# Bias rows copied into PSUM by ScalarE, the gain tables read as 32-row slices, and the order of VectorE and ScalarE changed in and ahead of the loop

## The reference

```
# layer 0
kx   = modulated_linear(x, s, k_aff_w, k_aff_b, k_w, k_b)     # per token 16 heads of 32
A    = softmax(kx kx^T / sqrt(32))                            # 16 x 16 heads, within a token
x    = x + modulated_linear(A kx, s, o_aff_w, o_aff_b, o_w, o_b)
# modulated_linear: w_mod = w * style, each row scaled to length 1; x w_mod^T + b
# layer 1, ln(x, g, b) is a layer norm with the gain and bias rows that the token's ids pick
h    = ln(ln(x, pw_g[pid], pw_b[pid]), cp_g[cid], cp_b[cid])
t, s = ln(x, tm_g[cid], tm_b[cid]), ln(x, ms_g[sid], ms_b[sid])
m, n, r = x + mlp_ln(memory), x + mlp_ln(noise), x + mlp_ln(resource)   # one row per batch
cat  = [w0*h, w1*t, w2*m, w3*n, w4*r, w5*s],  w = softmax(aw)
x    = x + ln(silu(cat @ int_W1 + int_b1) @ int_W2 + int_b2, int_g, int_be)
```

## Time and profile before

| | us |
|---|---|
| median of 3 runs | 938.13 |
| lowest, highest | 935.24, 938.22 |
| the profiled execution, its own time | 936.79 |
| its span, first to last instruction | 935.0 |
| TensorE busy | 876.8 (94%) |
| VectorE busy | 698.0 (75%) |
| GpSimd busy | 592.5 (63%) |
| ScalarE busy | 450.6 (48%) |

### The profile page before, as it was taken

The page is one execution under the profiler, slowest core; times in us unless marked ns, Lnnn a source line. Parts: engine busy times, 40 slices in busy tenths (PEclk is TensorE's granted clock), DMA queues, the critical chain, the costliest instruction groups (busy, mean ns, idle before and its releaser), DMA issues.

```text
span 935.0 us, 19902 instructions
## 1 busy us (share of the span) xinstructions
PE 876.8 (94%) x7518; PEld 789.8 (84%) x7566; DVE 698.0 (75%) x1129; ACT 450.6 (48%) x790; POOL 592.5 (63%) x742
## 2 busy tenths in 40 slices
PE   5876798999999999999999999999999999999987
PEld 5744697988989898998989898998979898999886
DVE  3679867778697777778787777778787777768642
ACT  3565336454544546454544645454544645453421
POOL 2267797766566675756576675856676675857551
PEclk9987799999999999999999999999999999999999
DMA  8951232422333232323334242323334242222110
GB/s 291 414 203 33 70 97 69 119 56 93 97 110 111 81 108 68 108 54 104 99 91 130 69 119 69 90 50 116 102 84 122 68 117 64 93 53 85 35 46 23
DMA packets 101871, 93.78 MB, mean 100 GB/s; under 512 B 72720, under 2 KB 75024, under 8 KB 100112
## 3 DMA queue, kind: packets, MB, share of 16 engines
q1 hardware_dynamic: 91984, 67.93, 24.0%
q0 software_dynamic: 4608, 16.78, 6.5%
q10 hardware_dynamic: 5184, 7.79, 2.7%
HBM read 67.83 MB, written 8.39 MB: 82 GB/s over the span
## 4 chain that ended last, share of the span: by engine, by line
PE 50%; DVE 26%; issue 9%; ACT 7%; another core or an unknown queue 4%; POOL 2%; DMA 2%; ACTq 1%; DVEq 0%; SPq 0%; POOLq 0%
PE acc L368 30%; PE tok L368 12%; PE att L368 3%; PE xp L511 3%; PE xp L368 2%; DVE norm L1280 2%; DVE ytmp L1266 2%; DVE SE L1195 2%; DVE small L1199 1%; DVE SE L1222 1%; DVE SE L1210 1%; DMA p_kb<-in_kb 1%; ACT pgb L795 1%; DVE alo L1228 1%
## 5 line engine op out<-in xcount | busy, mean ns | idle before, releaser
L1476 POOL TENSOR_TENSOR xlo<-xraw,xhi 128x512 fp32r<-128x512 f32 x32 | 46.8, 1464 | 104.8 <-ACT xhi L736 104.8
L1530 POOL TENSOR_TENSOR op1l<-ytmp,op1h 128x512 fp32r<-128x512 f32 x64 | 84.2, 1316 | 31.1 <-ACT op1h L824 30.7
L368 PE MATMUL acc<-op1h,W1th 128*128 128x256 f32 x256 | 80.2, 313 | 10.9 <-POOL op1l L1530 10.9
L368 PE MATMUL acc<-op0h,W1xh 128*128 128x256 f32 x256 | 77.2, 301 | 1.5 <-DVE op0l L1252 1.5
L824 ACT CAST op1h<-ytmp 128x512 fp32r<-128x512 f32 x64 | 39.7, 621 | 78.6 <-DVE ytmp L1266 78.6
L368 PE MATMUL acc<-op1h,W1hh 128*128 128x256 f32 x256 | 77.5, 303 | 0.0
L368 PE MATMUL acc<-op1l,W1th 128*128 128x256 f32 x256 | 77.4, 302 | 0.0
L368 PE MATMUL acc<-op1h,W1tl 128*128 128x256 f32 x256 | 77.3, 302 | 0.0
L368 PE MATMUL acc<-op0h,W1sh 128*128 128x256 f32 x256 | 73.7, 288 | 0.0
L368 PE MATMUL acc<-op0h,W1xl 128*128 128x256 f32 x256 | 73.0, 285 | 0.0
L368 PE MATMUL acc<-op0l,W1xh 128*128 128x256 f32 x256 | 73.0, 285 | 0.0
(11 more groups left out here) (248 smaller groups left out, 3201.2 us busy)
## 6 DMA issues: line engine op xcount, KB each, us to landing
xsq<-in_x SPq DMA_DIRECT2D x32, 256.0 KB, 4.3
xb<-in_x SPq DMA_DIRECT2D x32, 256.0 KB, 2.9
out<-xb SPq DMA_DIRECT2D x32, 256.0 KB, 2.0
xraw<-in_xT SPq DMA_DIRECT2D x31, 256.0 KB, 4.3
BD<-q SPq DMA_DIRECT2D x124, 64.0 KB, 2.1
BD<-v SPq DMA_DIRECT2D x124, 64.0 KB
ring<-in_k_wT ACTq DMA_DIRECT2D x12, 256.0 KB
ring<-in_o_wT ACTq DMA_DIRECT2D x12, 256.0 KB
```

The lines of the kernel that those rows point to most:

```text
L368: return e.matmul(o, a, b, start=start, stop=True, skip_group_check=True)
L1476: e.tensor_tensor(xlo[:, :, :], xraw[:, :, :], xhi[:, :, :].bitcast(F32), ALU.subtract).then_inc(s["xlo"], 1)
L1530: e.tensor_tensor(op[slot]["l"][:, :, half(g)], four(ytmp[YT[n, g][0]]), op[slot]["h"][:, :, half(g)].bitcast(F32), ALU.subtract).then_inc ...
```

## The change

1. **Bias rows.** In the 32 `W2_part`s and in `proj(g)` of the 14 even groups from 4 on, the bias matmul with `selT` is gone. ScalarE copies the row, held in SBUF for all partitions (`kb`, `b2`), into the PSUM bank ahead of the matmuls (`bias_q`, `bias_2`), which then all accumulate. The other 18 `proj`s keep theirs.
2. **Gain tables.** `gain_tables` and `GT` are gone. `gains` takes the 32 partitions of `tab` and of `OH` that hold its table: matmuls over 32 rows of the array.
3. **Steps with weights.** ScalarE's `z_copy(pb)` stands ahead of `mod_hi`, VectorE's `product(pb, "t")` ahead of `mod_lo`.
4. **Ahead of the loop.** VectorE's `vectors_end` is cut in two and moved behind `e_second(1)`; the three batch-row tables L are made by ScalarE straight from PSUM; `split3` for `PT` moves into step 1, between `q_T(b)` and `a_lo(a)`; its inputs `rp` and `t1` lie in other buffers, so groups 2 and 3 are loaded earlier and `gint` later. On TensorE `values(1)` comes ahead of `vec_T`, `a_T(1)` ahead of `tables_mnr`. GpSimd makes the later batches' row scales (`demod(., 1)`) ahead of the loop.

```diff
             def proj(g, kts=range(4)):
+
                 o = tok[1 if g else 0]
...
+                    elif on_bias:
+                        e.wait_ge(s["sd"], g // 2 - 1)
...
-                    three(o[:, :], xhi[:, kt, :], xlo[:, kt, :], WL["k", "h"][:, kt, :], WL["k", "l"][:, kt, :], kt == 0)
+                    i = three(o[:, :], xhi[:, kt, :], xlo[:, kt, :], WL["k", "h"][:, kt, :], WL["k", "l"][:, kt, :], kt == 0 and not on_bias)
                 if kts[-1] == 3:
-                    mm(o[:, :], selT[:, 0, :], tab[:, :]).then_inc(s["A"], 1)
+                    if not on_bias:
+                        i = mm(o[:, :], selT[:, :], tab[:, :])
+                    i.then_inc(s["A"], 1)
...
                 for c in range(4):
-                    i = mm(o[:, c * 128:c * 128 + 128], GT[n][:, c * 128:c * 128 + 128], OH[(g // 2) % 2][:, half(g)], start=(c == 0))
+                    i = mm(o[:, c * 128:c * 128 + 128], tab[q, c * 128:c * 128 + 128], OH[(g // 2) % 2][q, half(g)], start=(c == 0))
...
-            def W2_last(g):
-                W2_part(g, (2, 3))
-                mm(tok[g % 2][:, :], selT[:, 1, :], tab[:, :]).then_inc(s["W2"], 1)
...
+            def bias_q(g):
+
+                e.wait_ge(s["ql"], g)
+                e.copy(tok[1][:, :], kb[:, :]).then_inc(s["sd"], 1)
+
+            def bias_2(g):
+
+                if g % 2 == 0:
+                    e.wait_ge(s["x1"], min(g + 3, NG))
+                elif g < NG - 1:
+                    e.wait_ge(s["ql"], min(g + 4, NG))
...
+                e.copy(tok[g % 2][:, :], b2[:, :]).then_inc(s["sw"], 1)
...
+                if k > 1:
+                    z_copy(pb)
                 if mod:
                     mod_hi(*mod, (0, 1))
-                if k > 1:
-                    z_copy(pb)
                 prod_hi(pb, "t")
...
                     prod_hi(pb, "s")
+                    if more:
+                        bias_q(a + 2)
...
                     z_make(a)
+                    bias_2(pa)
                     sum_part(b, "S", "Sc")
                     if more:
                         q_hi(a + 2)
                     exponential(b)
+                    bias_2(pb)
...
+            vectors_norm()
+            e_T(1)
+            x_one(0)
+            e_second(1)
             vectors_end()
-            x_one(0)
-            e_T(1)
             q_lo(2)
-            e_second(1)
-            for n in "mnr":
-                table_rows(n)
...
-            split3(1, rp[:, :], PT[:, :])
...
+                product(pb, "t")
                 if mod:
                     mod_lo(*mod, (0, 1))
-                product(pb, "t")
...
                     q_T(b)
+                    if k == 1:
+                        split3(1, rp[:, :], PT[:, :])
                     a_lo(a)
```

More of the change, by code:

```diff
@@ L622, in _ @@
             proj(2)
+            values(1)
             vec_T()
-            values(1)
             z_T(0)
+            a_T(1)
             tables_mnr()
-            a_T(1)
             scores(2)
@@ L679, in _ @@
                     u_T(a)
-                W2_first(pa)
-                W2_first(pb)
-                W2_last(pa)
+                W2_part(pa, (0, 1))
+                W2_part(pb, (0, 1))
+                W2_part(pa, (2, 3))
                 if front:
@@ L686, in _ @@
                     scores(a + 2)
-                W2_last(pb)
+                W2_part(pb, (2, 3))
                 if front:
@@ L911, in _ @@
             q_hi(2)
+            e_first(1)
             z_make(0)
-            e_first(1)
             split_x(3)
             squares(3)
+            sum_part(1, "AV", "AVc")
             e.wait_ge(s["vTr"], 1)
-            e.copy(vT[:, :, :].rearrange("p a b -> p (a b)"), xp[XP["vT", 0][0]][:, :]).then_inc(s["vT"], 1)
+            for i, n in enumerate("mnr"):
+                j = e.activation(L[n][:, :, 0:24].rearrange("p k (r c) -> p k r c", c=8)[:, :, :, 0:4],
+                                 four(xp[XP["vT", 0][0]])[:, :, 32 * i:32 * i + 4].unsqueeze(2).to_broadcast([128, 4, 3, 4]), ACT.Copy, scale=w7[:, 2 + i:3 + i])
+                j.then_inc(s["LB"], 1)
             e.wait_ge(s["c_rs"], 16)
@@ L963, in _ @@
                 u_make(pb)
+                if k == 1:
+                    e.wait_ge(s["tA"], 2)
+                    e.copy(t2[:, 256:512].bitcast(BF16), rp[:, :]).then_inc(s["tp"], 1)
                 if not front:
@@ L993, in _ @@
                     e_first(b)
+                if not front:
+                    bias_2(pa)
+                    bias_2(pb)
                 silu(k - 1, 0)
@@ L1126, in vectors, with vectors_norm @@
                 e.bn_aggr(mv, bs).then_inc(s["lnA"], 1)
-            def vectors_end():
+            def vectors_norm():
                 r = slice(0, 96)
@@ L1132, in vectors_end @@
                 e.tensor_scalar(h2[r, :], h2[r, :], mv[:, 0:1], small[r, 75:76], ALU.subtract, ALU.mult).then_inc(s["h2"], 1)
+            def vectors_end():
+                r = slice(0, 96)
                 e.wait_ge(s["h2"], 3)
@@ L1302, in _ @@
             demod_eps(0)
-            gain_tables()
             one_hot(0)
@@ L1329, in _ @@
             less_max(1)
+            vectors_norm()
+            e_T(1)
+            x_one(0)
+            e_second(1)
             vectors_end()
-            x_one(0)
-            e_T(1)
             q_lo(2)
-            e_second(1)
-            for n in "mnr":
-                table_rows(n)
+            a_sum(1)
             q_T(2)
-            x_weights(1, range(4))
-            a_sum(1)
-            x_weights(2, (0, 1))
+            x_weights(1, (0, 1))
             a_lo(1)
-            x_weights(2, (2, 3))
-            v_stats(0)
+            x_weights(1, (2, 3))
+            x_weights(2, range(4))
             product(0, "t")
             v_T(2)
+            v_stats(0)
+            x_one(1)
+            x1_lo(0)
             e.wait_ge(s["Pm"], 7)
```

135 lines of the change are left out of this document (62 added, 73 removed).

## The result

The forecast was 922.5 us with a range of 901 to 936. The changed kernel took 940.45 us in the median of 20 runs (937.62 to 941.61), the one before 937.3 (934.17 to 938.25), also 20 runs. The ratio is 1.0041 [1.0032, 1.0051]: slower by 0.4%, outside the range and on the other side. The profiled execution has a span of 938.6 us, the one of before 935.0. Executions of one kernel also differ by the clock they are granted: in the last set of 22 of the kernel before, spans are 933.8 to 937.8 us where the mean clock is 0.966 to 0.969 and 929.8 to 934.5 where it is 0.971 to 0.979; the trace of before (0.968) is of the first kind.

A forecast was written before the change was run, and what follows sets the result against it. TensorE, busy 94% of the span, was taken as the bound. Terms -19.5 (t product), -10.6 (bias rows), +21 (gains) and -5.5 (front) sum to -14.6 from 936.79; with 1.3 to the median, forecast 922.5 us, range 901 to 936.

The forecast's parts named there:

- The t product: Six steps with weights: op1l waits vanish, gain 6 x 3.37 = 20.2, given back 0 to 3, taken 0.7: -19.5 us.
- The clock's share of it: Steps with weights: 3.37 us is twice the wait; the rest is the clock, at 1.2 GHz for some 4 us.
- The bias rows: 32 W2_parts and 14 projs each lose a 0.23 us matmul, wholly on TensorE: -10.6 us; ScalarE copies taken as 0.
- The 32-row slices: 96 gains calls, each losing 0.22 us by changing array shape there and back: +21 us.
- The rival of free shapes: In gains, 32-row shapes cost nothing: 901 us; chance 0.20.
- the one of dearer shapes: In gains, the array empties and weights load uncovered, 0.55 us a call: 954 us, times from 937; chance 0.12.
- Ahead of the loop and in step 1: VectorE work leaves the path to values(1) and values(2); TensorE starts earlier: -5.5 us, range -8.5 to -2.
- The sum: Whole kernel: all terms added, -19.5 - 10.6 + 21 - 5.5 = -14.6 us.
- Rival (c): Six steps with weights: the t gain does not come, a short wait still lowers the clock: 942 us; chance 0.08.

The follow-up runs named there:

- kernel 1: The kernel before with only the gains calls reading 32-row slices (GT copies still made): 948.38 us, ratio 1.0121.
- kernel 3: The kernel before with only the t product ahead of the low parts and z_copy(pb) ahead of mod_hi: 932.78 us, ratio 0.9952.
- kernel 5: The changed kernel with split3 in step 1 moved behind product(pb, "h"): 937.6 us, ratio 1.0002 to the kernel before.
- kernel 7: The changed kernel with gains over full rows, proj biases as matmuls again and split3 behind product(pb, "h"): 927.11 us, ratio 0.9902 to the kernel before.
- kernel 11: The kernel before with only the W2 bias rows by ScalarE and the t product ahead of the low parts: 928.93 us, ratio 0.9929.
- kernel 10: kernel 7 with, in steps with weights, a_hi ahead of u_make and q_T behind alo and mod_lo(2, 3): 936.45 us, ratio 1.0006 to the kernel before.

## Why the forecast was wrong, step by step

**The t product (forecast -19.5).** This was the step that failed most. The first half was right: the waits for `op1l` vanished. The size was taken as the whole of 3.37 us per step, "given back 0 to 3, taken 0.7" in all; this is the term that failed. Measured alone it is 1.1 us in step 8, 5.6 over steps 2 to 15 (734.96 - 729.39) and 5.3 by the medians. In the changed kernel the excess of the six steps with weights over plain ones shrank from 22.9 to 11.1 us, but the slices alone had brought it to 11.9 (kernel 1): beside them the t product won next to nothing. The forecast priced each part on the kernel before, as if the others were not there.

In kernel 3 the row up to `alo` was not far off. With its times moved by 1.30 us, so that the t product starts at 484.14 as in the forecast, `alo` ends at 494.97 and TensorE is there at 494.04, where the forecast had 494.8 and 494.3: a wait of 0.99 instead of up to 0.5. Behind it came one that the forecast did not name, 0.59 us for `Wol` (in steps 4, 8 and 12), and each wait cost some 0.16 us more than its bracket. That is 1.9 of the 2.3 us that came back in step 8.

In the changed kernel the same row also stretched. VectorE and GpSimd in step 8, before and, in the second fence, in the changed kernel:

```profile
491.51 1.52 DVE L1062 SCALAR_TENSOR_TENSOR ring<-ring,styl,dmb 128x512 f32<-128x512 f32 x2
...
493.44 1.30 POOL L1501 TENSOR_TENSOR xb<-xb,ob 128x512 f32<-128x512 f32 x1 [3.09 <-DMA xb<-in_x]
```

```profile
486.25 2.87 DVE L1093 TENSOR_TENSOR Wol<-ring,Woh 128x512 fp32r<-128x512 f32 x2
...
493.52 2.48 DVE L1087 SCALAR_TENSOR_TENSOR ring<-ring,styl,dmb 128x512 f32<-128x512 f32 x2
495.93 1.08 DVE L1193 STREAM_TRANSPOSE q<-qt 128x512 uint32<-128x512 uint32 x1
496.87 0.66 DVE L1248 TENSOR_TENSOR alo<-xp,ahi 128x512 fp32r<-128x512 f32 x1
...
494.18 1.28 POOL L1520 TENSOR_TENSOR xb<-xb,ob 128x512 f32<-128x512 f32 x1 [2.18 <-DMA xb<-in_x]
```

`mod_weights` took 1.52 us while GpSimd idled, and 2.48 beside GpSimd's addition; `Wol` 2.87 instead of 2.36. In step 7 of the same execution the two stand a little otherwise. VectorE, GpSimd and TensorE of the changed kernel:

```profile
439.57 1.41 DVE L1087 SCALAR_TENSOR_TENSOR ring<-ring,styl,dmb 128x512 f32<-128x512 f32 x2
...
440.35 1.80 POOL L1520 TENSOR_TENSOR xb<-xb,ob 128x512 f32<-128x512 f32 x1 [2.31 <-DMA xb<-in_x]
...
442.65 0.39 PE L368 MATMUL xp<-OH,tab 32*128 32x128 bf16 x4 [0.32 <-DVE alo L1248]
```

Here GpSimd's addition began behind the second `ring` and was itself the one to stretch, to 1.80 us. In steps 3, 8 and 11 the two `ring` took 2.46 to 2.48 us and the wait for `alo` is 1.31 or 1.32; in steps 4, 7 and 12 they took 1.41 or 1.42 and it is 0.32 to 0.36. So 1.0 of the 1.31 is this stretch. It is not what spoilt the gain, though: step 7 took 53.95 us and step 3, with the stretch, 54.13, since a wait of 0.38 for `ytmp` follows in step 7, and in five of kernel 3's six steps the two `ring` took 1.40 or 1.41 and the wait for `alo` was 0.97 to 1.00 all the same.

The Trainium skill, GPSIMD Engine Reference, 1. Specifications, says that GpSimd shares its SBUF interface with VectorE and contends with VectorE instructions that have two SBUF inputs. The rows agree: `Wol`, `ring` and the 3.80 us of kernel 5 read two operands from SBUF, while the products and `alo`, with one operand in PSUM, take 0.65 to 0.70 throughout the changed kernel. No run here took the GpSimd instruction away; the test is the six steps of one trace.

**The clock's share of it.** The forecast held that half of the 3.37 us was the clock and would come back in full. In kernel 3 it did (a mean granted clock of 1.00 in all six steps, 0.97 before), and still only 1.1 was left. It may even be most of what was won: kernel 3's eight executions span 929.4 to 933.5 us at a clock of 0.975 or above, and those of the kernel before that were granted 0.971 or more span 929.8 to 934.5, in another set on the same chip. The 0.16 us beside a bracket can be read in kernel 7: its `gains` at 491.00 stands 1.26 us behind the last matmul at 489.74, where 0.12 is the pitch and 0.98 the bracket, so this wait cost about 0.16 more than its bracket.

**The bias rows (forecast -10.6).** The size of one matmul, 0.23, was right. That all 46 are "wholly on TensorE, the bound" was wrong: the one at the end of `W2_part(pb)` covered a wait for `last_norm(pb)`. A plain step won 0.22 from the W2 rows. The plain step of the changed kernel is 50.83 + 1.48 (slices) - 0.22 (W2) - 0.2 = 51.89; the last term is what is left for the k rows, near their 0.23, and no run measured them alone. Over steps 2 to 15 that is about -6 instead of -9.7. The end won 1.2 where +0.8 was forecast; what did it was not settled.

**The 32-row slices (forecast +21).** Right for a call: 0.25 measured where 0.22 was taken from the earlier trace rows, which makes +20.7 in steps 2 to 15. Wrong as a sum for the kernel before: alone they cost 9.2 us there, since in the steps with weights they shortened a wait and kept the clock up. The rival of free shapes and the one of dearer shapes (0.55 a call) both fall, although the measured time lies within the 937 to 954 of the latter. The rule of the Trainium skill, TensorEngine Tiling (Array Packing), Key Properties, that a change of tiling mode drains TensorE, agrees with the rows, where a change costs 0.08 to 0.12 us.

**Ahead of the loop and in step 1 (forecast -5.5).** `values(1)` came 2.6 us earlier (70.06 for 72.66), in the range given, but of this only 0.4 was left at the transposes of step 1, where a new wait of 5.73 for `pgb` stands. The wait for `e_second(2)` shrank from 5.65 to 1.25 and the one for `op1l` behind it came, as forecast, with 1.34 rather than some 4. The first `W1_part` began at 109.47 instead of 113.16, 3.7 us won. Then the sentence failed that "`split3` in step 1 fills time in which VectorE waited for `ahi`". VectorE of the changed kernel:

```profile
112.73 0.89 DVE L1099 TENSOR_TENSOR p_rp<-p_rp,p_t 128x512 f32<-128x512 f32 x1
...
118.46 1.63 DVE L1106 SCALAR_TENSOR_TENSOR PT<-p_rp,cst,p_t 128x512 bf16<-128x512 f32 x1
120.01 0.68 DVE L1248 TENSOR_TENSOR alo<-xp,ahi 128x512 fp32r<-128x512 f32 x1
```

The five operations took 7.3 us, with GpSimd's split of W1 and three more of its operations beside them, and TensorE waited 4.34 for `alo`. Its price was never put into the sum. Kernel 5 shows that of the 4.34 us only 1.3 stay won at the end of step 1 (159.81 to 158.51) when this wait is gone, or 2.0 counted from the first `W1_part` (109.47 and 110.12), and kernel 11 that the old order is as good, within the variation there. That the one-off work of VectorE and GpSimd in front of `values(3)` is what binds there, in any order, is how I read the two; no run shortened that work.

**The sum.** Off by 7.7 in the t product, 3.7 in the bias rows, 2.2 in the slices, 6.5 in front and -2.0 at the end: 18.1 of the 18.2 us between -14.6 and the measured +3.6 of the span. Two of these shares depend on the order of counting: with the slices first, as kernel 1 measured them, they cost 9.2 us in steps 2 to 15 instead of 18.5, and the t product won some 0.4 instead of 19.5. The 6.5 in front holds up to 2 us of variation. The errors of the t product and of the bias rows have one root: a wait or a matmul that goes was priced by its own length, without the wait that stood ready behind it, and parts that meet at the same wait were added up.

Rival (c), with 942 us and a chance of 0.08, came nearest to the measured 940.45, since it gave the t product nothing. Its condition did not come, though: the waits for `op1l` went and the clock stayed up. The bias rows and the work in front also won less than it says. So its closeness is in part luck. The forecast also has two slips: 936.79 - 14.6 with the 1.3 to the median makes 923.5 and not 922.5, and its own terms put end to end give 908 to 937 and not 910 to 934. Neither reaches 940.45.

## What to carry to other kernels

When a wait is removed at a place where several engines are nearly level, price the gain by the next row that ends there, with room for its instructions to stretch, and not by the wait; here 1.1 us of 3.4 stayed. An instruction on the bound engine can cover another engine's lateness: before counting it as won, look at what the instruction behind it would wait for. Parts of a change that end at the same wait are not to be added: price them together, or measure each alone. Between large matmuls, four small ones that address 32 rows were dearer here, by 0.25 us, than full ones padded with zeros; gathering them so that the shape seldom changes was not tried.

## What the hardware showed that was not expected

- Going from 128x128 to 32x128 and back cost 0.25 us on TensorE (0.124 per change), and 0.083 for each further change between single matmuls. The matmuls themselves were not faster: the four of a call take 0.39 us in either shape.
- Behind a wait of 1.25 us in kernel 1 TensorE went on at 0.12 us per 256-column matmul (2.4 GHz), behind one of 1.71 us before at 0.21 (1.2 GHz) for some 4 us. But it also went on at 2.4 GHz behind 2.00 us in kernel 3 and 2.02 in kernel 10, and fell behind 2.24 and 2.31 there; the length of the wait alone does not decide. A delay of TensorE in front of a wait was free in kernel 1, and better than free: its step 8 took 53.76 us, with six dearer calls, instead of 54.20.
- VectorE instructions with two operands in SBUF and GpSimd's stretch one another, and in these rows the one that starts second is the one that stretches: in step 8 GpSimd's addition starts 0.01 us ahead of a `ring` (494.18, 494.19), takes 1.28 us, and the `ring` 1.82; in kernel 7's step 7 it starts 0.06 us behind one (434.98, 434.92), takes 1.82, and the `ring` 0.73. In kernel 5 one instruction of 0.69 took 3.80 beside four GpSimd subtractions in a row.
